# A vision tower on one core: who normalises, when weights are rounded and cleared, one load, constants, and mixing in quarters

## What is computed

```python
h = tok(x); h = concatenate([cls_tok, h])
h = h + L0_attn(layernorm(h))      # causal, rotary, low rank
h = h + L0_ffn(layernorm(h))       # 32 experts, all of them, softmax gates
h = h + L1_attn(layernorm(h))      # 12 heads of 64, relative positions
h = h + L1_ffn(layernorm(h))       # 8 experts, top 1
h = h + L2_attn(layernorm(h))      # random features ("performer")
h = h + L2_ffn(layernorm(h))       # attention, MLP, then 4 experts, top 2
h = h + L3_attn(layernorm(h))      # 8 bit input, integer softmax
h = h + L3_ffn(layernorm(h))       # attention or pooled mixing, then MLP
# in L3_ffn, per image: scores = sigmoid(normed @ Wr + br)
#   w = scores / (sum(scores) + 1e-6);  pooled = sum(w * normed)
#   mix_out = (normed + scores * pooled) @ Wm + bm
#   merged = where(attn_mask, attn_out, mix_out)
```

## Time and profile before

| | us |
|---|---|
| median of three runs | 3123.96 (3122.16 to 3128.41) |
| the profiled execution, its own time | 3126.66 |
| its span, first to last instruction | 3124.9 |
| PE busy | 2918.5 |
| DVE busy | 2097.0 |
| ACT busy | 1074.7 |
| POOL busy | 607.2 |

### The profile page before, as it was taken

How to read it: one execution, slowest core, us unless ns; L and a number is a source line. 1 busy time by engine, 2 the same in 40 slices (tenths; PEclk the granted TensorE clock), 3 DMA queues, 4 the chain that set the end, 5 groups by cost and what they waited for, 6 DMA issues and landing times. The chain is left out here.

```text
span 3124.9 us, 56497 instructions
## 1 busy us (share of the span) xinstructions
PE 2918.5 (93%) x19995; PEld 2678.2 (86%) x19995; DVE 2097.0 (67%) x5299; ACT 1074.7 (34%) x2140; POOL 607.2 (19%) x763
## 2 busy tenths in 40 slices
PE   9899999999999999999998998897989889978888
PEld 7779999999999999999997888675768879867767
DVE  3867677777776777777777766234457657877876
ACT  2533333333333333333334333213435333334433
POOL 1312121212121112111203000112213102121440
PEclk9989999999999999999999999898999989989888
DMA  3001000000000000000000000471000010000000
GB/s 135 37 18 36 36 20 34 36 36 18 36 36 36 18 36 36 36 18 36 18 31 8 2 2 2 147 220 38 1 11 8 13 54 18 11 1 16 23 18 17
DMA packets 24461, 105.56 MB, mean 34 GB/s; under 512 B 4455, under 2 KB 9463, under 8 KB 19086
## 3 DMA queue, kind: packets, MB, share of 16 engines
q1 hardware_dynamic: 22654, 99.62, 9.2%
q0 software_dynamic: 1584, 3.30, 0.3%
HBM read 98.32 MB, written 6.64 MB: 34 GB/s over the span
## 5 line engine op out<-in xcount | busy, mean ns | idle before, releaser
L896 ACT ACTIVATE hid<-bank,dat 128x384 f32<-128x384 f32 (+1 forms) x912 | 555.7, 610 | 1146.5 <-PE bank L586 1031.1
L861 PE MATMUL bank<-w,hid_hi 128*128 128x384 f32 x2964 | 860.2, 361 | 2.2 <-DVE y_tok L912 1.6
L863 PE MATMUL bank<-w,hid_lo 128*128 128x192 f32 x2964 | 746.3, 252 | 0.0
L863 PEld LDWEIGHTS bank<-w,hid_lo 128*128 128x128 f32 x2964 | 571.7, 193 | 1.7
L861 PEld LDWEIGHTS bank<-w,hid_hi 128*128 128x128 f32 x2964 | 562.2, 190 | 5.4 <-issue 3.7
L930 DVE TENSOR_TENSOR hid_lo<-hid,hid_hi 128x384 fp32r<-128x384 f32 (+1 forms) x912 | 539.9, 592 | 31.5
L927 DVE CAST hid_hi<-hid 128x384 fp32r<-128x384 f32 (+1 forms) x912 | 340.9, 374 | 126.8 <-ACT hid L896 125.5
L953 DVE SCALAR_TENSOR_TENSOR h_tok<-bank,gate,h_tok 128x192 f32<-128x192 f32 x416 | 173.5, 417 | 248.9 <-PE bank L863 244.6
L586 PE MATMUL bank<-xa_hi,w_hi 128*128 128x384 f32 (+1 forms) x912 | 324.8, 356 | 7.6 <-DVE w_lo L739 4.6
L586 PE MATMUL bank<-xa_lo,w_hi 128*128 128x384 f32 (+1 forms) x912 | 323.3, 354 | 0.0
L586 PE MATMUL bank<-xb,w_lo 128*128 128x384 f32 (+1 forms) x912 | 322.5, 354 | 0.0
(11 more groups left out here) (361 smaller groups left out, 4379.9 us busy)
## 6 DMA issues: line engine op xcount, KB each, us to landing
raw<-in_L_exp SPq DMA_DIRECT2D x36, 1344.0 KB, 5.7
w_e<-in_L_exp SPq DMA_DIRECT2D x20, 576.0 KB, 4.0
w_e<-in_L_exp SPq DMA_DIRECT2D x20, 384.0 KB
pix<-in_pixels SPq DMA_DIRECT2D x6, 832.0 KB, 10.4
w_e<-in_L_exp SPq DMA_DIRECT2D x20, 195.0 KB
raw<-in_L_mlp SPq DMA_DIRECT2D x2, 1344.0 KB, 5.7
wp_raw<-in_L_att SPq DMA_DIRECT2D x1, 2304.0 KB, 8.2
route_rows<-in_rows_clear SPq DMA_DIRECT2D x1, 2000.0 KB, 23.0
```

Source lines behind the costliest of these rows:

```text
L861: nc.tensor.matmul(o[:, 0:2 * D], hid_hi[k % 2][:, m, c], w2[j][:, m, :], start=m == 0, stop=False)
L863: ins = nc.tensor.matmul(o[:, 0:D], hid_lo[k % 2][:, m, c], w2[j][:, m, 0:D], start=False, stop=m == HC - 1)
L896: nc.scalar.activation(hid[(6 * k + m) % 3][:, 0:128 * nt], bank[4 + (6 * k + m) % 4][:, 0:128 * nt], func, bias=bias).then_inc(s["h_act"] ...
```

## The change

Seven edits:

1. In affine phases DVE normalises blocks 1 and 2 (eight tiles) and ACT blocks 0 and 3.
2. Where the others of the phase say `late` (both feature phases with `attention_weights(parts=True)` and full rank in L2 and L3, and the two with expert weights spread), ACT rounds both weight pieces behind the four evictions. Elsewhere the later pieces stand one each ahead of an eviction.
3. `inner` is cut in two: the reciprocal and nine tiles ahead of the first `spread`, four tiles behind it.
4. The clearing of `v_x` (2 x 1536 + 128 columns) goes behind the instruction that raises `att_ready`, with a semaphore `v_clear` of its own, for which ACT waits before the first value eviction. This is in the attentions of L0, L1, L2 and L3.
5. The load of the first two experts of L2_ffn waits for the split of the MLP's weights ahead of it in place of the phase.
6. In the last turn of the mixed attention PE runs ten products of constants ahead of its wait for the split result.
7. `shares`, `raise`, `add` and the last product of `keep` are each four instructions of 208 columns.

```diff
@@ -415,7 +417,7 @@
-            on_dve = (2,) if ln else (1, 2)
+            on_dve = (1, 2)
             on_act = [i for i in range(4) if i not in on_dve]
@@ -427,6 +429,7 @@
             pieces = [p for o in others for p in o.get("high", ())]
+            late_weights = any(o.get("late") for o in others)
             ident = shp[:, SHAPE_COLS["ident"]]
@@ -498,17 +501,24 @@
                             .then_inc(s["root"].sem, 1)
-                    piece(0)
+                    late = norm_of is None or late_weights
+                    if not late:
+                        piece(0)
                     for i in on_act[1:]:
                         normalise(i)
-                    piece(1)
+                    if not late:
+                        piece(1)
                     high(0)
-                    piece(2)
-                    piece(3)
+                    for i in range(1, 4):
+                        if not late:
+                            piece(i + 1)
+                        high(i)
+                    if late:
+                        piece(0, 1)
                 else:
-                    high(0)
-                for i in range(1, 4):
-                    high(i)
+                    for i in range(4):
+                        high(i)
@@ -546,11 +556,12 @@
-            def inner(dve):
-                dve.wait_ge(s["root"].sem, b["root"] + 2)
-                nc.vector.reciprocal(once[:, 2, :], once[:, 1, :]).then_inc(s["dve_step"].sem, 1)
+            def inner(dve, part):
+                if part == 0:
+                    dve.wait_ge(s["root"].sem, b["root"] + 2)
+                    nc.vector.reciprocal(once[:, 2, :], once[:, 1, :]).then_inc(s["dve_step"].sem, 1)
                 dve.wait_ge(s["dve_step"].sem, b["dve_step"] + 1)
-                for t in range(TILES):
+                for t in range(9) if part == 0 else range(9, TILES):
                     nc.vector.tensor_scalar(keep[:, t, :], norm_of[:, t, :], mv[:, t, 0:1], once[:, 2, t:t + 1],
@@ -741,7 +752,7 @@
             if spread:
-                return dict(sync=sync), dict(high=[lambda act: high(act, 0), lambda act: high(act, 1)]), dict(b, low=low)
+                return dict(sync=sync), dict(high=[lambda act: high(act, 0), lambda act: high(act, 1)], late=True), dict(b, low=low)
             return dict(sync=sync), dict(gpsimd=gpsimd), b
@@ -1328,13 +1339,18 @@
+                if not cleared:
+                    nc.gpsimd.memset(pads[-3], 0.0).then_inc(v_clear, 1)
+            if not cleared:
+                clearings[0] += 1
             def low(dve):
...
                 return dict(sync=sync, high=[lambda act: high(act, 0), lambda act: high(act, 1)], gpsimd=gpsimd,
-                            low=[low] if cleared else [])
+                            low=[low] if cleared else [], late=not low_rank)
             return dict(sync=sync, scalar=scalar, gpsimd=gpsimd)
@@ -1364,13 +1380,15 @@
                 for m in [xs[:, p, :, :].rearrange("p j (m s) -> p (j m) s", s=32)[:, :, SLOT:32] for p in range(3)] \
-                        + [p[:, :, SLOT:32] for p in p_t] + [v_x[:, :], rel_a[:, :, 20:32]]:
+                        + [p[:, :, SLOT:32] for p in p_t] + [rel_a[:, :, 20:32]]:
                     nc.gpsimd.memset(m.bitcast(F32) if m.dtype == F32R else m, 0.0)
...
                                  0.0).then_inc(s["att_ready"].sem, 1)
+                nc.gpsimd.memset(v_x[:, :], 0.0).then_inc(v_clear, 1)
+            clearings[0] += 1
             return dict(sync=sync, gpsimd=gpsimd, high=[lambda act, p=p: high(act, p) for p in range(4)],
@@ -1542,24 +1560,30 @@
                 ti = slice(n * i, n * i + n)
-                both = [128, 2, n]
+                m, h = 8, n // 2
+                parts = [(c, slice(n * i + h * y, n * i + h * y + h), slice(h * y, h * y + h),
+                          slice(16 * i + m * y, 16 * i + m * y + m)) for c in range(2) for y in range(2)]
                 if step == "shares":
...
                         pool.wait_ge(mix["s_all"], 16)
-                    nc.gpsimd.tensor_tensor(shares, of_turn(feat, i), s_b[:, ti].unsqueeze(1).to_broadcast(both),
-                                            ALU.mult).then_inc(mix["shares"], 1)
+                    for c, tc, sc, mc in parts:
+                        ins = nc.gpsimd.tensor_tensor(shares[:, c, sc], feat[:, c, tc], s_b[:, tc], ALU.mult)
+                    ins.then_inc(mix["shares"], 1)
                     pool.wait_ge(mix["shares"], i + 1)
...
                     pool.wait_ge(mix["pooled"], i + 1)
-                    for c in range(2):
+                    for c, tc, sc, mc in parts:
                         ins = nc.gpsimd.tensor_tensor(
-                            by_images(shares[:, c, :]), by_images(s_b[:, ti]),
-                            pooled[:, c, 16 * i:16 * i + 16].unsqueeze(2).to_broadcast([128, 16, SLOT]), ALU.mult)
+                            by_images(shares[:, c, sc]), by_images(s_b[:, tc]),
+                            pooled[:, c, mc].unsqueeze(2).to_broadcast([128, m, SLOT]), ALU.mult)
                     ins.then_inc(mix["raised"], 1)
...
                 elif step == "add":
-                    nc.gpsimd.tensor_tensor(of_turn(feat, i), of_turn(feat, i), shares, ALU.add).then_inc(mix["added"], 1)
+                    for c, tc, sc, mc in parts:
+                        ins = nc.gpsimd.tensor_tensor(feat[:, c, tc], feat[:, c, tc], shares[:, c, sc], ALU.add)
+                    ins.then_inc(mix["added"], 1)
                     pool.wait_ge(mix["added"], i + 1)
@@ -1568,9 +1592,9 @@
                     pool.wait_ge(mix["kept"], i + 1)
-                    nc.gpsimd.tensor_tensor(of_turn(feat, i), of_turn(feat, i),
-                                            shares[:, 0, :].unsqueeze(1).to_broadcast(both), ALU.mult)\
-                        .then_inc(mix["mixed"], 1)
+                    for c, tc, sc, mc in parts:
+                        ins = nc.gpsimd.tensor_tensor(feat[:, c, tc], feat[:, c, tc], shares[:, 0, sc], ALU.mult)
+                    ins.then_inc(mix["mixed"], 1)
                     pool.wait_ge(mix["mixed"], i + 1)
@@ -1620,6 +1644,7 @@
             ready = s["att_ready"].at
+            cleared_by = clearings[0]
@@ -1736,6 +1761,10 @@
                         pe.wait_ge(wide_in["out_ready"], 1)
+                    if cfg.mix and i == NI - 1:
+                        pe.wait_ge(s_free.sem, s_free_at + 16)
+                        keep_clock(bank[4], 10)
                     pe.wait_ge(s["o_split"].sem, b["o_split"] + i + 1)
@@ -1849,6 +1878,8 @@
                     j = t % 2
+                    if t == 0:
+                        act.wait_ge(v_clear, cleared_by)
                     for v in range(halves):
@@ -2205,10 +2236,14 @@
+                        for o in others if i == 0 else ():
+                            if "first" in o:
+                                o["first"](dve, 0)
                         spread(i)
...
                             if "first" in o:
-                                o["first"](dve)
+                                o["first"](dve, 1)
                     elif name == "rope":
@@ -2279,7 +2314,9 @@
         experts_phase(1, a["L2_mlp"], "L2m_b1", "L2m_b2", y_tok, ACT.Gelu, w, stats_of=y_tok)
-        load, split, w = expert_weights(4, a["L2_exp"], ("phase_done", 3 * len(phases)), spread=True)
+        mlp_divided = signals["w_split"].at
+        load, split, w = expert_weights(4, a["L2_exp"], ("w_split", mlp_divided), spread=True)
         features_phase(n_tok, load, split, ln="ln_L2f2", norm_of=y_tok, gate=("L2_g", 4))
...
         experts_phase(4, a["L2_exp"], "L2e_b1", "L2e_b2", y_tok, ACT.Gelu, w, g, onto=h_tok, stats_of=h_tok)
```

4 lines of the change are left out of this document (3 added, 1 removed).

## The result

The changed kernel takes 3102.8 us (median of four executions, 3094.6 to 3103.1) against 3124.0 (3122.2 to 3128.4): the ratio is 0.9925, 95% interval 0.9913 to 0.9937. That is 21.2 us in the medians where 14.1 were forecast. The direction was right and the size was a third short.

A forecast was written before the change was run, and what follows sets the result against it. TensorE, busy over nine tenths of the span, was taken as the bound, so only its waits could give. Gains less losses summed to 14.1 us, from 3123.96 to 3109.9 us; range 3102 to 3118.

The forecast's parts named there:

- Five of the feature phases: Before the attentions of L0, L1, L2, L2_ffn and before the four experts: gains of 0.8, 0, -3.1, 0.8 and 6.5 us.
- the quantising: In L3, the clearing of `v_x`, moved later, would stall a VectorE tensor_scalar: a loss of 1.2 us, at most 2.8.
- The two of L3_ffn: Feature phases before L3_ffn's attention and before the last MLP: gains of 2.5 us and 0.
- L2's loss: Features of L2's attention: both roundings behind the last eviction delay GpSimd's `wp_lo` and `q_t`, costing 3.1 us, possibly 4.6.
- The largest term: Features before the four experts: no wait for the load, no rounding or four tiles ahead of TensorE's second block; gain 6.5 us.
- the 3.71 of waiting goes: Before the four experts, ScalarE would no longer stand still 3.71 us for the weights, as their load is issued earlier.
- `inner`: L2_ffn's attention: nine tiles and the reciprocal move into VectorE's idle time; gain 2.0 us (0.3 to 2.9); in L3_ffn's 0.1.
- quarters: Mixing in L3_ffn's attention: shorter GpSimd products hold VectorE less, 3.1 us at the splits and 0.6 at the spreads.
- constants: Ahead of the last mixing in L3_ffn's attention: ten products keep TensorE's clock up for the 24 products behind; gain 2.0 us.
- rival B: TensorE's clock stays up into the last MLP's features, whose constants take 3.86 instead of 6.75 us: 3107.0 us; chance 0.25.
- the sum for L3_ffn's attention: Mixing by smaller products 3.7, products ahead of the last mixing 2.0, cut inner norm 0.1: 5.8 us gained.
- the stretches that were forecast at 0: Stretches for which no gain or loss was forecast, such as the attentions of L0 and L3 and the four experts.

## Why the prediction was right, and where it was short

*Features.* Five of the feature phases and the quantising were forecast within 0.7. The two of L3_ffn gave 1.2 more each (3.65 for 2.5, 1.20 for 0): in both TensorE's constants took 1.2 less by the clock (5.65 for 6.90, 5.55 for 6.75). L2's loss was 2.95 for 3.1, at the place and by the chain that were named.

*The largest term had the right size and half a reason.* 6.4 for 6.5. I credited the earlier load ("the 3.71 of waiting goes"); the run without it shows that the late rounding takes the wait away by itself, and that the load edit gives nothing here.

*`inner`, quarters, constants* measure about 2.3 (1.8 to 3.3 of TensorE's waiting), 3.6 and 2.1 to 2.4 for 2.0, 3.7 and 2.0. The constants also shortened the next phase by 1.0 to 1.2, which was rival B with under half its size. In three of the variants the clock did stay up into that phase (its constants 3.86 long, its features 15.6 instead of 17.25), and there the last MLP took 63.0 instead of 60.2: what B would have given beyond the changed kernel is more than taken back just behind it. What I drew for B from the Trainium skill (page "TensorE: Matmul & The Clock Gate", section "What's actually happening": the half rate is the default, activity lifts it) came true in those three, and in the changed kernel only in part (its constants 5.55).

*The step that failed* is the sum for L3_ffn's attention: 3.7 + 2.0 + 0.1 = 5.8, where 10.76 came. Every edit in it was sized well. The sum left TensorE's clock in the middle of the attention as it was before, though the trace of before shows three waits of 2.95 to 3.75 us there, each with a stretch near 0.5 behind it; I had looked at the clock only at the end of the attention. In the changed kernel two of the three stretches are missing and one is shorter, less a new one later: 4.4 of the 5.0 us. The rest is `inner`, at 0.8 for 0.1, and the constants, at 2.4 for 2.0, less the quarters, at 3.2 for 3.7. Constants in the three waits brought 7.5. With that much possible, the range would have had to reach from 3109.9 down to 3102.4, and with B to 3099.5. The same left-out clock is in the stretches that were forecast at 0 and gave 2.7 together; which waits gave that was not followed.

*How much of the 21.2 is the change?* As far as the medians of four and six executions show, all of it: 21.2 and 22.3, at alignments that differ from one execution to the next. The edits themselves, priced one by one, add up to about what was forecast. The rest comes through the clock. A likely reason, not tested by itself, is that TensorE waits 14.8 us less in the changed kernel, so the clock has fewer places to fall. It is not the price of any one edit, and a single trace can show far more or less of it.

*What stays open:* how the place of a wait on the clock's grid decides, at 2.3 us, whether the clock falls; how much of the gain a longer set of executions would keep; and the share of the moved clearing in the 1.9 of the first attention.

## What to carry to other kernels

Put the granted clock beside every wait of TensorE before summing, not only beside those that the edit touches: the wait costs its length, and then possibly half of a stretch of 3 to 7 us behind it. Where it can't be removed, fill it: three products on a free bank, ahead of the semaphore wait, gave 7 to 8 us here for two lines. And price an edit by a stretch in which the clock is held, or by the waits of TensorE, not by the length of a stretch in two traces: the same quarters measured 0.3, 3.6 and 10.6 us, and only the middle number is theirs.

## What was unexpected of the hardware

The same instructions took 142.1 or 152.6 us in one stretch, and 171.0 or 177.2 in another, by where their start met the clock's grid. L1's attention took 295.3 in one trace and 301.7 in another of kernels with the same code up to there. A clock that stays up in one phase is often paid back in the next: with `inner` cut, six traces had the features of L2_ffn's attention at 18.5 and 171.0 behind them, and six had them at 17.2 to 17.7 and 177.0 to 177.3 behind. On VectorE, a 64x416 subtraction takes 2.22 beside a GpSimd product of 832 columns, 0.90 beside one of 208, and 0.59 alone; a tensor_scalar on one element is not held by a clearing that holds one on 2496 for 0.96.
